# Last layer's input work moved into the scatter pass, one unit of 128 nodes per group

## The reference

```python
edge_index = jnp.stack([src, dst])
h = jnp.maximum(_layernorm(x), 0.0)
x = x + rgcn_twice(h, edge_attr_42, ...)          # 10 relations, two rounds
h = jnp.maximum(_layernorm(x), 0.0)
x = x + typed_conv(h, edge_type_3, edge_weight)   # 3 relations
h = jnp.maximum(_layernorm(x), 0.0)
x = x + sage_twice_bn_fc(h)                       # batch norm over all nodes, then h @ fcW.T + fcb
h = jnp.maximum(_layernorm(x), 0.0)
# last layer, a continuous filter
g = h @ W_in2f
Wij = (ssp(edge_attr_20 @ W_filt1 + b_filt1) @ W_filt2 + b_filt2) * edge_weight[:, None]
agg = segment_sum(g[dst] * Wij, src, n)
x = x + (ssp(agg @ W_out1 + b_out1) @ W_out2 + b_out2)
```

## Time and profile before

| | |
|---|---|
| median of 3 runs | 17679.55 us (17678.54 to 17693.12) |
| the profiled execution, its own time | 17666.72 us |
| its span in the profile | 17665.0 us |
| mean granted PE clock | 0.62 of full speed |
| busy: PE, DVE, ACT, POOL | 45%, 39%, 18%, 61% of the span |
| dense stage 5 | 13868 to 14192 us, the batch norm's statistics included |
| scatter pass, first to last scatter | 14212.6 to 17374.1 us |

### The profile page before, as it was taken

The page is one execution under the profiler, slowest core; times in us unless marked ns, Lnnn a source line. Parts: engine busy times, 40 slices in busy tenths (PEclk is TensorE's granted clock), DMA queues, the critical chain, the costliest instruction groups (busy, mean ns, idle before and its releaser), DMA issues.

```text
span 17665.0 us, 179568 instructions
## 1 busy us (share of the span) xinstructions
PE 7873.9 (45%) x36107; PEld 6273.0 (36%) x36108; DVE 6843.6 (39%) x28057; ACT 3221.2 (18%) x6961; POOL 10730.4 (61%) x10236
## 2 busy tenths in 40 slices
PE   5633333623333333333333333333333577777777
PEld 3333333322222223332332322222222455555555
DVE  8522222244444423323322222344544344444443
ACT  3422222300000000000000000000000144444443
POOL 0266666365555546666566666666666268888882
PEclk8755555856666555555555555555555577777775
DMA  2333333411111131111111111233333266666665
GB/s 102 125 88 89 89 88 88 175 47 53 54 54 53 53 104 53 52 52 51 51 46 46 47 47 47 60 87 85 87 86 87 66 113 118 117 117 118 117 118 122
DMA packets 1122539, 1438.17 MB, mean 81 GB/s; under 512 B 211981, under 2 KB 737444, under 8 KB 1122316
## 3 DMA queue, kind: packets, MB, share of 16 engines
q0 software_dynamic: 536912, 792.85, 21.0%
q1 hardware_dynamic: 531700, 613.30, 11.9%
q10 hardware_dynamic: 53748, 30.36, 0.6%
HBM read 1101.27 MB, written 334.40 MB: 81 GB/s over the span
## 4 chain that ended last, share of the span: by engine, by line
another core or an unknown queue 29%; issue 22%; DVE 21%; DMA 10%; POOL 6%; PE 5%; ACT 3%; DVEq 2%; ACTq 1%; SPq 0%; POOLq 0%
DMA agg_dram<-acc,sum_row 9%; DVE tab_s L1950 5%; POOL agg_dram L887 5%; DVE scratch L1950 4%; DVE xn_h L1958 3%; DVE scratch L1920 3%; DVE acc L1906 2%; DVE rows L1818 1%; PE ps L1604 1%; POOL scratch L901 1%; ACT hT_s L1009 1%; PE ps L1361 1%; PE ps L1561 1%; PE ps L1562 1%
## 5 line engine op out<-in xcount | busy, mean ns | idle before, releaser
L901 POOL DMA_INDIRECT scratch<-table_dram,row_st x4160 | 3966.4, 953 | 2541.5 <-ACT row_st L1040 1269.3
L901 POOL DMA_INDIRECT rows<-table_dram,row_st x4160 | 3964.0, 953 | 2321.5 <-issue 1247.3
L1361 PE MATMUL ps<-tab_s,rows 128*128 128x128 f32 x8320 | 1906.8, 390 | 3028.0 <-issue 1274.0
L1361 PE MATMUL ps<-scratch 128*128 128x128 f32 x8320 | 1829.5, 390 | 2873.1 <-DMA scratch<-table_dram,row_st 1247.8
L887 POOL DMA_INDIRECT agg_dram<-acc,sum_row x1664 | 2654.5, 1595 | 529.2 <-issue 391.2
L1361 PEld LDWEIGHTS ps<-tab_s,rows 128*128 128x128 f32 x8320 | 1694.4, 294 | 3214.8 <-issue 2149.0
L1361 PEld LDWEIGHTS ps<-scratch 128*128 128x128 f32 x8320 | 1617.8, 289 | 3058.3 <-issue 2119.2
L1906 DVE TENSOR_TENSOR acc<-ps,acc 128x128 f32 x2080 | 608.6, 293 | 4575.8 <-remote 4054.7
L1950 DVE TENSOR_SCALAR scratch<-ps,rw_st 128x128 f32<-128x128 f32 x3328 | 1114.3, 401 | 338.4 <-issue 227.4
L1920 DVE SCALAR_TENSOR_TENSOR scratch<-iota,rw_st,ps 128x128 f32<-128x128 f32 x2496 | 715.2, 343 | 1355.3 <-remote 873.9
L1950 DVE TENSOR_SCALAR tab_s<-ps,rw_st 128x128 f32<-128x128 f32 x3328 | 1112.2, 401 | 330.3 <-issue 247.0
(11 more groups left out here) (229 smaller groups left out, 10600.9 us busy)
## 6 DMA issues: line engine op xcount, KB each, us to landing
scratch<-in_src_row SPq DMA_DIRECT2D x832, 256.0 KB
table_dram<-tab_s POOLq DMA_DIRECT2D x200, 640.0 KB, 3.2
scratch<-type_dram SPq DMA_DIRECT2D x416, 256.0 KB
scratch<-in_dst_row SPq DMA_DIRECT2D x416, 256.0 KB
rows<-table_dram,row_st POOLq DMA_INDIRECT x4160
scratch<-table_dram,row_st POOLq DMA_INDIRECT x4160
scratch<-table_dram SPq DMA_DIRECT2D x416, 64.0 KB
agg_dram<-acc,sum_row POOLq DMA_INDIRECT x1664
```

The source lines that it names most:

```text
L901: pool.indirect_dma_start(row_banks[bank][:, u, :], None, table_dram[k], bass.IndirectOffsetOnAxis(ap=row_st[:, bank, u:u + 1], axis=0)).t ...
L1361: mm = pe.matmul(ps[bank][:, q * P:(q + 1) * P], rows[:, u, :], hot[:, u, :], start=u % QUAD == 0, stop=u % QUAD == QUAD - 1)
```

## The change

Stage 5's dense work is done for two superblocks (`FIRST`) ahead of the pass. The other 23 superblocks are 92 units of 128 nodes; unit g is done in group g of the pass, spread over its quads, and its table goes out at the start of group g + 2. On PE the sums of a quad now go to two PSUM banks in turn instead of four, so that two banks are free for the unit; `sums` and `hotT` move out of `acc`, which the units still read. SP's loop over the groups has three groups written out at either end of the units, the other engines' loops one. The chip checks in addition that no window lies further ahead than the units have come (`furthest`). In the stages of `FLOWS`, DVE now waits for its own `flow_keep` and `flow_init`. Parts of the diff:

```diff
+FIRST = 2
+    n_units = min(4 * max(nsb - FIRST, 0), max(ngroups - 3, 0) // 4 * 4)
+    first_sb = nsb - n_units // 4
+    furthest = (4 * first_sb - 3 + (4 * (LAG - 1) if checked else 0)) * P
...
+        hotT = flat(rows)[:, 2 * BANK:4 * BANK].rearrange("p (b e) -> p b e", b=2)
...
+        sums = scratch[:, sums_at:sums_at + GROUP * P].rearrange("p (q b) -> p q b", q=4)
...
+        def with_units(e, body):
+            body(0, True, False)
+            with e.Fori(0, n_units - 1) as i:
+                body(i + 1, True, True)
+            body(n_units, False, True)
+            with e.Fori(0, ngroups - n_units - 1) as i:
+                body(i + (n_units + 1), False, False)
```

SP, at the head of each group:

```diff
+                    def unit_load(g, t):
+                        sp.wait_ge(s_x_new, so_far(reps, 5, has_x, t) + 1)
+                        settle(sp)
+                        sp.dma_start(xs[:, 0, :], x_unit[2]...).then_inc(s_x_in, 16)
+                    def unit_store(g, t):
+                        sp.wait_ge(s_x_new, so_far(reps, 5, has_x, t) + 1)
+                        settle(sp)
+                        sp.dma_start(x_unit[3]..., xn[:, 0, :]).then_inc(s_x_out, 16)
+                    def unit_table(g, t, again):
+                        sp.wait_ge(c_evac, units_before(reps) + t + 3)
+                        settle(sp)
+                        sp.dma_start(table_unit..., kept[:, 0:P]).then_inc(c_out[0], 16)
...
+                        def group(g, loads, stores, tables, landed):
+                            t = sp.snap(r * n_units + g)
+                            if landed:
+                                sp.wait_ge(c_out[0], units_before(reps) * 4 + t * 16 - 16)
+                            if loads:
+                                unit_load(g, t)
+                            if stores:
+                                unit_store(g, t)
+                            if tables:
+                                unit_table(g, t, again)
+                            settle(sp)
                             win = windows(sp, g)
```

ACT, PE and DVE, by quad (`new`: this group has a unit; `old`: the group before had one):

```diff
+                    def unit_y(g, t):       # act: yT <- acc, Identity
+                    def unit_sd(t):
+                        act.wait_ge(s_var, so_far(reps, 5, has_ln, t) + 1)
+                        act.activation(nrm[:, 0, 1:2], nrm[:, 0, 0:1], ACT.Sqrt).then_inc(s_sd, 1)
+                    def unit_h(t):          # act: h <- xn, Relu, waits for s_nrm
+                    def unit_hT(t):         # act: hT_s <- ps[3], waits for s_hT_mm
+                    def unit_evac(t):       # act: kept <- ps[3], waits for c_mm
                             for q in range(4):
+                                if new and q == 0:
+                                    unit_y(g, t)
                                 act.wait_ge(pick_mm, n0 + (q + 3))
                                 act.wait_ge(msg_ready, n0 + (q + 3))
                                 act.activation(picked[:, q % 2, :], ps[5][:], ACT.Copy).then_inc(pick_ready, 1)
                                 filter_terms(act.snap(r * nq + g * 4 + (q + AHEAD)), q % 2)
+                                if old and q == 0:
+                                    unit_hT(act.snap(t - 1))
+                                if old and q == 1:
+                                    unit_evac(act.snap(t - 1))
+                                if new and q == 2:
+                                    unit_sd(t)
+                                if new and q == 3:
+                                    unit_h(t)
                                 act.wait_ge(sums_free, n0 * 4 + 4 * (q + 1))
                                 act.wait_ge(mm_done, n0 + (q + 9))
-                                act.activation(sums[:, q, :], ps[q][:], ACT.Copy).then_inc(add_done, 1)
+                                act.activation(sums[:, q, :], ps[q % 2][:], ACT.Copy).then_inc(add_done, 1)
...
-                pe.wait_ge(add_done, base + (q + 1))
+                pe.wait_ge(add_done, base + (q + 3))
...
+            def unit_update(t):             # pe: ones x fcb, yT x fcw into ps[2]
+            def unit_turn(t):               # pe: h x ident into ps[3], waits for s_h
+            def unit_table(t):              # pe: hT_s x win into ps[3], waits for s_hT
+                                quad_products(base, q)
+                                if old and q == 0:
+                                    unit_table(pe.snap(t - 1))
+                                if new and q == 0:
+                                    unit_update(t)
+                                if new and q == 3:
+                                    unit_turn(t)
...
+            def unit_x(t):                  # dve: xn <- ps[2] + xs, bn_stats, bn_aggr, variance + eps
+            def unit_scales(t):             # dve: waits for s_sd, reciprocal, -mean / std
                             filter_quad(r, g, dve.snap(turn * 4 + q), base, q, terms_sum)
+                            if new and q == 1:
+                                unit_x(t)
+                            if new and q == 2:
+                                unit_scales(t)
```

The check at the start, and the waits of `flow_keep` and `flow_init`:

```diff
+                step(dve.tensor_reduce(reps_f[:, 2:3], rel_dst[:], AX.X, ALU.max))
+                step(dve.tensor_scalar(reps_f[:, 2:3], reps_f[:, 2:3], furthest + 0.5, None, ALU.is_gt))
+                step(dve.tensor_tensor(reps_f[:, 0:1], reps_f[:, 0:1], reps_f[:, 2:3], ALU.add))
...
+                dve.wait_ge(s_keep, so_far(reps, k, has_src, t) + 2)
...
+                dve.wait_ge(s_init, so_far(reps, k, has_root, t) + 2)
```

More of the change, by code:

```diff
@@ L76, in build, with steps_of @@
     n_feat = 20
+    far = 1 << nwin.bit_length()
+    n_units = min(4 * max(nsb - FIRST, 0), max(ngroups - 3, 0) // 4 * 4)
+    first_sb = nsb - n_units // 4
+    def steps_of(p):
+        return first_sb if p["src"] == "bn" else nsb
     def turns(k, flag):
-        return nsb * sum(bool(flag(p)) for j, p in enumerate(DENSE[:k]) if j and j not in FLOWS)
+        return sum(steps_of(p) * bool(flag(p)) for j, p in enumerate(DENSE[:k]) if j and j not in FLOWS)
     def has_src(p): return p["src"] != ""
@@ L101, in chunks @@
     def chunks(k):
-        return nsb * sum(n_chunks(p) for j, p in enumerate(DENSE[:k]) if j and j not in FLOWS)
+        return sum(steps_of(p) * n_chunks(p) for j, p in enumerate(DENSE[:k]) if j and j not in FLOWS)
     nblocks = ngroups // BLOCK
@@ L555, in lane_uses @@
         def lane_uses(k, v):
-            return 1 + nsb * sum((4 // LANES if is_wide(p) else v == 0) for j, p in enumerate(DENSE[:k])
-                                 if has_table(p) and j and j not in FLOWS)
+            return 1 + sum(steps_of(p) * (4 // LANES if is_wide(p) else v == 0) for j, p in enumerate(DENSE[:k])
+                           if has_table(p) and j and j not in FLOWS)
         def wait_lane(e, k, i, j):
@@ L793, in _ @@
                                 load_sources(same_ready, n0 + q, g, q)
+                        if n_units:
+                            at = lambda g: (g < n_units, 0 < g <= n_units, 1 < g <= n_units + 1, 2 < g <= n_units + 2)
+                            for g in range(3):
+                                group(g, *at(g))
+                            if n_units > 3:
+                                with sp.Fori(0, n_units - 3) as i:
+                                    group(i + 3, True, True, True, True)
+                            for g in range(max(n_units, 3), n_units + 3):
+                                group(g, *at(g))
+                        rest = n_units + 3 if n_units else 0
+                        if ngroups - rest:
+                            with sp.Fori(0, ngroups - rest) as i:
+                                group(i + rest, False, False, False, False)
+                    with sp.Fori(0, reps) as r:
+                        sp.wait_ge(win_ready, reps * 6 + r + 1)
+                        settle(sp)
+                        filter_loads(r)
                         for q in range(AHEAD):
@@ L1461, in run_pass @@
                     else:
-                        with pe.Fori(0, ngroups) as g:
-                            group(g)
+                        with_units(pe, group)
             pe.wait_ge(type_ready, 1)
@@ L1993, in filter_pass, with group @@
                     terms_sum(dve.snap(r * nq), 0)
-                    with dve.Fori(0, ngroups) as g:
+                    def group(g, new, old):
                         turn = dve.snap(r * ngroups + g)
```

108 lines of the change are left out of this document (87 added, 21 removed).

## The result

The changed kernel takes 18609.8 us, the median of 4 runs (18589.0 to 18622.6), against 17686.3 us of the kernel before beside it (17678.5 to 17702.4): a ratio of 1.052, 95% interval 1.051 to 1.054. The profiled execution has a span of 18604.4 us, 939.4 more than the 17665.0 of before.

The account below looks back on a forecast made before the run. POOL's scatters were taken to bound the pass, at 30.4 us a group of four quads. The terms -269.6 + 2.3 + 1113 = +846 us, on the median 17679.6, gave 18525 us; 8 in 10 between 17950 and 18850.

Parts of the forecast that it names:

- (a): Dense stage ahead of the pass: 23 of 25 superblocks leave it, at 11.72 us each, 269.6 us less.
- (b): Lead check on the DVE chain: a reduction over 1664 columns and two one-column operations add 2.3 us.
- (c): Waits behind flow_keep and flow_init, two PSUM banks for four: 0, the waits at most +12 us.
- (d): Units in 92 of 104 groups of the pass: 42.5 us a group against POOL's 30.4, +1113 us.
- Rival (1): Only two table loads a group in the pass: about 31 us a group, about 17470 us, faster; chance 0.12.
- q=0: First quad of a unit group: terms, hT copy, table product, update, pick, first product: 8.9 or 11.7 us.
- q=1: Second quad: terms, table evacuation, features late behind SP's wait, first product: 10.2 or 12.2 us.
- q=2: Third quad: terms, Sqrt's load, Sqrt to scales, hotT held back, pick, first product: 9.95 or 11.7 us.
- q=3: Fourth quad: terms, Relu, the turn on PE, pick, first product: 8.3 or 10.2 us.
- (2): Rival: two loads every quad, but POOL stays the pass's bound; 267 us gained whole, 17412 us; chance 0.05.
- (3): Rival: the forecast's order with PE's clock high, 37.4 us a group, 18050 us; within the forecast's 0.82 chance.
- (4): Rival: the lead check fails, 98 rounds of every pass, 1.7 seconds; excluded by the inputs.

Follow-up runs that it names:

- run 1: The changed kernel with the table set of Exp and Ln named behind the unit's Sqrt: 17432.1 us, ratio 0.986 to the kernel before.
- run 2: The kernel before, with two table loads added to every quad's terms in the pass and no dense work moved: 17687.5 us, ratio 1.000.
- run 3: The changed kernel with the table store moved behind the loads of a group's first quad, table loads kept: 18257.2 us, ratio 1.032.
- Run 5: The changed kernel with the unit's Sqrt and reciprocal replaced by an Ln and an Exp on ACT: 17592.8 us on a second chip, ratio 0.985.
- run 7: The changed kernel with unread products added in PE's pauses: 18388.6 us on the second chip, ratio 1.031, 18230 us scaled to the first chip.
- run 8: The changed kernel with run 3's edit and the unit's Sqrt ahead of its quad's terms: 18056.8 us on the second chip, ratio 1.012.
- runs 1 and 4: The second of these is the changed kernel with the edits of run 1 and run 3 together: 17417.9 us, ratio 0.985.

## Why the prediction held

**The sum.** Predicted 18525 us (+846 against the profiled execution), measured 18609.8 (+939 in span, inside the range). The 93 us by the prediction's own terms:

| term | predicted | measured |
|---|---|---|
| (a) 23 superblocks | -269.6 | -262.7 from the batch norm to the first scatter |
| (b) lead check | +2.3 | the reduction took 1.89 us again; part of the next row |
| (c) waits, banks, ports | 0 (0 to +12) | +12.0 up to the batch norm, the check included |
| (d) the pass | +1113 | +1190.3 |
| sum | +846 | +939.4 (the terms add up to +939.6) |

**(a)** is right. Most of the 6.9 us by which it is short are the start of the pass: from the clearing MEMSET to the first scatter 26.6 us in place of 20.4. The loads in the first terms do that, which the prediction had left out; run 1, without them, takes 20.6 (13935.01 to 13955.6).

**(b), (c).** The 9.7 us beyond the check are no finding, since executions of the same code differ by more than that at the batch norm's first operation: the kernel before reaches it at 13868.1 us and run 2, the same kernel up to there, at 13880.1; the changed kernel at 13880.1 and run 3, the same up to there, at 13904.2. A price for the waits behind `flow_keep` could not be told from 0.

**(d), the tables.** The step that carried the forecast, that the builder takes a set for the function at hand and so gives Exp and Ln a load each, is what the trace shows: 835 loads where over 800 were named, 5.22 us for terms where 5.2 were. Run 5 shows the Sqrt to be the cause. That the builder takes a set for the function at hand fits all these counts, but how it chooses was only seen from outside. The Trainium skill ("ScalarE activation tables: per-element evaluation and per-set limits", section "Table sets in the compiler and the runtime") has the loads placed by the greedy longest run of a block; the measurement goes against that here: by that rule a unit group would have two loads, as the prediction says, and it has nine, and the last 12 groups, whose loop has no Sqrt at all, have eight each. Rival (1) was this rule's case, and run 1, which makes it by hand, took 17432 us where 17470 had been worked out for it.

**(d), the cycle.** The intervals of a unit group in us, as predicted with PE at full and at half clock, as measured, and with the pauses filled (run 7):

| interval | full clock | half clock | measured | run 7 |
|---|---|---|---|---|
| q=0 | 8.9 | 11.7 | 10.2 | 9.25 |
| q=1 | 10.2 | 12.2 | 10.9 | 10.2 |
| q=2 | 9.95 | 11.7 | 11.8 | 10.4 |
| q=3 | 8.3 | 10.2 | 10.35 | 9.55 |
| sum | 37.35 | 45.8 | 43.3 | 39.4 |

The sum lies where it was put, nearer the half-clock bound; the forecast took 42.5. The 0.8 us too few, times 92, are 74 of the 93 us by which the sum was short. The group's bounds held, and the value between them was a choice, so that it came within 0.8 us is in part luck. Single quads fit less well: q=2 and q=3 lie 0.1 and 0.15 us above their half-clock figures. q=0 stayed under its own, and in about a third of the groups the first product at its end came back at full clock (as at 15040.36, 1.12 us), at the end of the other three hardly ever.

The prediction also gives as the reason for the cycle that the first product writes the one PSUM bank. That is not what holds it: the wait is for the Ln's signal, 3.96 us after the Relu has read the bank. The sum is right all the same, since it follows the code's wait. Whether a signal behind the Relu would let the loads be hidden was not tried.

**The waits.** Each one named for a quad is in the timeline: the features behind SP's wait (run 3: 4.1 us a group), the Sqrt's chain to hotT (run 8: 3.9 us), ACT's hT and h ahead of the table product and the turn (1.53 and 1.83 us, not removed by themselves in any run). The 12 groups without a unit stayed near POOL's 30.4 us: 92 x 43.3 + 12 x 30.4 = 4348, the pass's first to last scatter being 4350.2.

**The rivals.** (2), loads that POOL hides, is half true, and run 2 shows the half: the loads by themselves are hidden whole, even with ACT 82% busy. What makes them cost is that they stand in series with the unit's waits, in a group whose steps go ACT to PE to ACT, and that PE's clock is low behind the waits. The point from which it decides was given as 33.3 us a group; runs 1 and 4, with the pass back at POOL's pace, lie on one side of it and run 8, at 35.35 us, on the other, each with the sign that follows. (3), a clock that stays high, was not the case, but run 7 reaches 39.4 us and 18230 on the way to its 18050. (4), a lead check that fails, would have shown in the pass, which ran once and with 92 units in it.

## What to carry to other kernels

Before a small operation is moved into a tight loop, look which activation table it wants: one Sqrt of 0.2 us turned 0 loads into 9 a group, and one line that names the set the loop lives on gave the whole 5% back and 1.4% on top. A loop that hides added work hides it only up to the bound's own interval, and additions that are each free (the loads, the unit's waits) may not be free together; so work out the cycle with all of them in series, quad by quad. Naming the set once ahead of the loop is not enough: here that load was followed at once by another. Where the move puts a wait at the head of a queue, as SP's table store ahead of the next features, put it behind the loads that others need first.

## What the runs showed of the hardware

A table load took 1283 ns whichever set was asked for, and the Exp behind it began 1.29 us after the load did (15000.75, 15002.04), so a switch cost 1.29 us. The Trainium skill ("ScalarE: Activation LUTs", section "What ACT_TABLE_LOAD costs") adds about 1.38 us of drain to the 1.28; this trace shows no such time on either side of a load.

Adding 2116 unread products to PE shortened a pass by 355 us, while the granted clock rose from 0.63 to 0.82 and ACT and POOL did the same work. I had the clock as a term, but did not expect that busy work would pay for itself.

Scatters were slightly shorter in the starved pass (mean 1570 ns, against 1598 in run 1, both with 5422 DVE operations), with the DMA engines 0.50 busy in place of 0.69. The difference is worth some 45 us over 1664 of them. It goes along with the DMA load, but the scatters also stand further apart in the starved pass, and no run tells the two apart.
